# Fused vision-text encoder block: second half's turning product ahead of a block of values, moments ahead of residual rows, bias products ahead of the gather

## The reference, cut to what matters

```python
h = concatenate([h, txt], axis=1)                  # (8, 96, 192)
x = layernorm(h)
q, k, v = split(x @ Wqkv_w + Wqkv_b)               # 12 heads of 16
attn = softmax(q @ (k / 4).T + causal_mask)
attn_output = (attn @ v) @ out_w + out_b
selection = softmax((x @ sel_w + sel_b) / temperature)[..., 1:]
idx = top_k(selection, 10)                         # ten tokens of each image
y = x; y[idx] += (attn_output * selection)[idx]
h = h + y
h = h + mixture_of_experts(layernorm(h))           # 16 routed experts and a shared one
```

## Time and profile before

| | |
|---|---|
| median of 3 runs | 221.13 us (220.51 to 221.18) |
| the profiled execution, its own time | 220.96 us |
| its span, first to last instruction | 219.1 us |
| TensorE busy | 209.3 us (95%), 1433 products |
| VectorE busy | 148.6 us (68%) |
| ScalarE busy | 117.1 us (53%) |
| GpSimd busy | 36.6 us (17%) |
| chain that ended last, by engine | PE 81%, DVE 9%, ACT 3%, DMA 2%, issue 2% |

### The profile page before, as it was taken

The page is one execution under the profiler, slowest core; times in us unless marked ns, Lnnn a source line. Parts: engine busy times, 40 slices in busy tenths (PEclk is TensorE's granted clock), DMA queues, the critical chain, the costliest instruction groups (busy, mean ns, idle before and its releaser), DMA issues.

```text
span 219.1 us, 4307 instructions
## 1 busy us (share of the span) xinstructions
PE 209.3 (95%) x1433; PEld 190.2 (87%) x1433; DVE 148.6 (68%) x413; ACT 117.1 (53%) x246; POOL 36.6 (17%) x63
## 2 busy tenths in 40 slices
PE   7999999999999997999999999999999999999993
PEld 3888999888899985686877997999999999999992
DVE  0188967873566463664477699878878787878773
ACT  2157944668643746525334667266555555555552
POOL 8011006543851044040031000000000000000000
PEclk9999999999999999999999999999999999999999
DMA  6998000000000000030000001546554544444203
GB/s 222 406 405 234 0 1 4 0 3 0 3 0 0 0 3 1 1 93 6 0 3 0 0 18 27 153 149 177 146 176 138 135 153 139 138 138 138 93 0 108
DMA packets 10081, 18.69 MB, mean 85 GB/s; under 512 B 1425, under 2 KB 4641, under 8 KB 10066
## 3 DMA queue, kind: packets, MB, share of 16 engines
q1 hardware_dynamic: 9344, 16.76, 24.3%
q10 hardware_dynamic: 722, 1.74, 2.1%
HBM read 17.85 MB, written 0.64 MB: 84 GB/s over the span
## 4 chain that ended last, share of the span: by engine, by line
PE 81%; DVE 9%; ACT 3%; DMA 2%; issue 2%; POOL 1%; ACTq 1%; DVEq 0%
PE bank L544 7%; PE bank L545 6%; PE bank L547 6%; PE bank L548 6%; PE bank L546 6%; PE bank L712 4%; PE bank L581 3%; PE bank L1043 3%; PE bank L1053 3%; PE bank L1049 3%; PE bank L1044 3%; PE bank L1045 3%; DMA rows<-in_rows 2%; PE bank L691 2%; PE bank L662 2%
## 5 line engine op out<-in xcount | busy, mean ns | idle before, releaser
L1408 ACT ACTIVATE hid_s<-hid 128x384 fp32r<-128x384 f32 x34 | 17.9, 525 | 25.6 <-DVE hid L1879 25.2
L1398 ACT ACTIVATE silu<-bank,expert_raw 128x384 f32<-128x384 f32 x34 | 19.7, 579 | 10.2 <-PE bank L548 10.1
L1861 DVE SCALAR_TENSOR_TENSOR gated<-bank,expert_raw,silu 128x384 f32<-128x384 f32 x32 | 19.5, 613 | 7.3 <-PE bank L548 7.0
L1885 DVE TENSOR_TENSOR hid_s<-hid,hid_s 128x384 fp32r<-128x384 f32 x34 | 18.6, 552 | 7.8 <-ACT hid_s L1408 7.7
L544 PE MATMUL bank<-tA,ug_w 128*128 128x384 f32 x68 | 23.1, 340 | 0.1
L545 PE MATMUL bank<-tA,ug_w 128*128 128x384 f32 x68 | 22.9, 337 | 0.0
L547 PE MATMUL bank<-tB,ug_w 128*128 128x384 f32 x68 | 22.9, 337 | 0.0
L546 PE MATMUL bank<-tA,ug_w 128*128 128x384 f32 x68 | 22.9, 337 | 0.0
L548 PE MATMUL bank<-tB,ug_w 128*128 128x384 f32 x68 | 22.9, 336 | 0.0
L1879 DVE TENSOR_TENSOR hid<-w_all,gated 128x384 f32<-128x384 f32 x28 | 15.4, 552 | 0.1
L1174 ACT ACTIVATE act<-bank,cols 128x256 f32<-128x256 f32 x24 | 11.1, 472 | 7.9 <-PE bank L566 4.4
(11 more groups left out here) (356 smaller groups left out, 547.8 us busy)
## 6 DMA issues: line engine op xcount, KB each, us to landing
w_all<-routing_weights SPq DMA_DIRECT2D x14, 384.0 KB, 3.7
expert_raw<-in_experts SPq DMA_DIRECT2D x17, 256.0 KB, 3.5
expert_raw<-in_experts SPq DMA_DIRECT2D x17, 97.0 KB, 1.9
patches<-in_patches SPq DMA_DIRECT2D x3, 384.0 KB, 7.6
ff_raw<-in_ff ACTq DMA_DIRECT2D x1, 768.0 KB, 7.5
kv_raw<-in_kv SPq DMA_DIRECT2D x1, 578.0 KB, 11.8
patch_w<-in_patch_w ACTq DMA_DIRECT2D x2, 288.0 KB, 4.1
ff_raw<-in_ff SPq DMA_DIRECT2D x1, 576.0 KB, 8.6
```

The source lines that it names most:

```text
L1398: a(silu[hf][:, :], bank[3 + 2 * hf][:, 0:H2N], ACT.Silu, bias=expert_raw[:, p, BU:BU + 1]).then_inc(s[f"silu{hf}"], 1)
L1408: a(hid_s[p][:, 0, H2N * hf:H2N * hf + H2N], hid[hf][:, :], ACT.Copy)\
L1861: v.scalar_tensor_tensor((hid if first else gated)[hf][:, :], bank[4 + 2 * hf][:, 0:H2N], expert_raw[:, p, BG:BG + 1], silu[hf][:, :], ALU ...
L1885: v.tensor_tensor(hid_s[p][:, 1, tok], hid[hf][:, :], f(hid_s[p][:, 0, tok]), ALU.subtract)\
```

## The change

- TensorE: the turn of the second half goes ahead of `token_rows(3)`; the two products of `avb_all` with `out_w` go from behind the mask products to ahead of the bias row of the gather; the two fillers named `hot` there are dropped.
- ScalarE: the two row copies of the second half are put between the read-outs of images 0, 1 and 2; the rounding of the second half goes ahead of the read-outs of image 3 and of the keys.
- GpSimd: both reciprocal square roots go ahead of both sums `hx`, and both sums now come after both halves' `xn`.
- VectorE: `down_lo(0, 0)` goes from ahead of `aq_blk` to behind `hotpT`.

```diff
-    "turn_h1": 1, "vk1": 0, "psel": 0, "pickT": 1, "pick": 1, "hot": 2, "xs": 2, "aq": 0, "as0": 0,
+    "turn_h1": 1, "vk1": 0, "psel": 0, "pickT": 1, "pick": 1, "hot": 0, "xs": 2, "aq": 0, "as0": 0,
@@ GpSimd
             for hf in range(2):
                 gp.wait_ge(s["mv2_done"], hf + 1)
                 rsqrt(ve2t, mv2t, rs2t, 2 * hf, 2 * hf + 2, 128, "rs_done")
-                gp.wait_ge(s["xn_done"], hf + 1)
+            gp.wait_ge(s["xn_done"], 2)
+            for hf in range(2):
                 gp.wait_ge(s["h_rows"], 2 * hf + 2)
                 b = slice(4 * hf, 4 * hf + 4)
                 g.tensor_tensor(hx[:, b, :], h[:, b, :], xn[:, b, :], ALU.add).then_inc(s["hx_done"], 1)
@@ TensorE
             turn_logits(0)
-            token_rows(3)
             pe.wait_ge(s["xn_done"], 2)
             turn_h(xn, 1, bank[4], bank[5], "hT_ps")
+            token_rows(3)
             keys(0)
@@ TensorE
             keep_busy("hot", bank[5])
             pe.wait_ge(s["av_done"], 8)
+            pe.wait_ge(d_aq, 16)
+            pe.wait_ge(s["avb_done"], 2)
+            for ch in range(2):
+                mm(bank[7][0:SLOTS, 0:DIM], avb_all[:, ch, :], out_w[:, ch, :], start=(ch == 0), stop=False,
+                   skip_group_check=True)
...
-            pe.wait_ge(d_aq, 16)
-            pe.wait_ge(s["avb_done"], 2)
-            for ch in range(2):
-                mm(bank[7][0:SLOTS, 0:DIM], avb_all[:, ch, :], out_w[:, ch, :], start=(ch == 0), stop=False,
-                   skip_group_check=True)
@@ ScalarE
             hi_of_turned(bank[0][:, 0:H2N], bank[1][0:FB, 0:H2N], H2N, slice(0, H2N), "hT_ps", 1)
-            image_rows(0)
+            image_rows(0, 0)
+            image_rows(0, 1)
             logits_out(0)
-            for b in range(HALF_IMG):
-                values_out(b)
+            values_out(0)
+            image_rows(1, 0)
+            values_out(1)
+            image_rows(1, 1)
+            values_out(2)
+            hi_of_turned(bank[4][:, 0:H2N], bank[5][0:FB, 0:H2N], H2N, slice(H2N, T2), "hT_ps", 2)
+            values_out(3)
             keys_chunk0(0)
-            hi_of_turned(bank[4][:, 0:H2N], bank[5][0:FB, 0:H2N], H2N, slice(H2N, T2), "hT_ps", 2)
-            image_rows(1)
             logits_out(1)
@@ VectorE
             keys_chunk1(1)
-            down_lo(0, 0)
...
+            down_lo(0, 0)
```

More of the change, by code:

```diff
@@ L1306, in values_out, with image_rows @@
                     .then_inc(s["av_done"], 1)
-            def image_rows(hf):
+            def image_rows(hf, i):
                 act.wait_ge(s["mv2_done"], hf + 1)
[L1311 to L1314, removed]
+                first = HALF_IMG * hf + i
+                a(h[0:IMG_TOK, first:first + 3:2, :], x1b[64 * i:64 * i + 64, 2 * hf:2 * hf + 2, :], ACT.Copy)\
+                    .then_inc(s["h_rows"], 1)
             hi_of_turned(bank[0][:, 0:H2N], bank[1][0:FB, 0:H2N], H2N, slice(0, H2N), "hT_ps", 1)
-            image_rows(0)
+            image_rows(0, 0)
+            image_rows(0, 1)
             logits_out(0)
-            for b in range(HALF_IMG):
-                values_out(b)
+            values_out(0)
[5 more added lines that the diff above has]
+            values_out(3)
             keys_chunk0(0)
-            hi_of_turned(bank[4][:, 0:H2N], bank[5][0:FB, 0:H2N], H2N, slice(H2N, T2), "hT_ps", 2)
-            image_rows(1)
             logits_out(1)
```

## The result

The changed kernel takes 218.93 us (median of six executions) where the kernel before takes 221.16: a ratio of 0.9898, with a 95% interval of 0.9881 to 0.9915.

What follows compares the result with a forecast made beforehand. TensorE was taken to bound the kernel, busy 95% of the span and 81% of the chain. Gains of 1.28 + 0.45 = 1.73 us gave 219.4 us median; own range 219.1 to 219.7, 8 in 10 from 218.8 to 220.3.

Steps and rivals of the forecast that it cites:

- The turn, 1.28 us: TensorE, second half: turning ahead of token_rows(3) removes waits, so token_rows(4) starts at 84.24 instead of 85.52, 1.28 us gained.
- The root: GpSimd: the second half's reciprocal root, no longer behind hx, starts at 78.04 instead of 78.36, 0.32 us earlier.
- The slack of the low part: VectorE's low part of the turn: ready at 83.26, needed by logits_keys(1)'s fourth product at 83.86, 0.6 us of slack.
- ScalarE's list, costing nothing: ScalarE: row copies before image 2's read-out and the rounding moved forward cost nothing, with 0.6 us of slack.
- The bias products and the fillers, 0.45 us: TensorE, marked tokens to scores: 0.68 us of products move ahead of the gather, fillers go; scores gain 0.45 us.
- down_lo, nothing: VectorE: down_lo(0, 0) behind hotpT takes 0.5 us, done at 99.0 before the maxima at 99.7, costing nothing.
- The lock on the port pair: VectorE and GpSimd: exclusive only for VectorE operations with two SBUF inputs; down_lo then costs its bare 0.5 us.
- GpSimd's sums hold VectorE: Rival, chance 0.05: hx and avb_all shut VectorE out of the turn's low parts; fourth product 1.53 us late, 222.2 us.
- One of the moved pieces takes part back: Rival, chance 0.12: down_lo's long form costs 0.6 us, or the root brings nothing, 0.32 us; 219.7 to 220.0 us.
- Only half takes: Rival, chance 0.08: psel, after the second logits, waits on something unmoved; only the fillers' 0.45 us remain, 220.7 us.
- More than the sum: Rival, chance 0.10: selection's short steps catch up and blocks lose joints of 0.04 us; 0.3 to 0.5 more, 219.0 us.
- The clock falls, 0.03: Rival, chance 0.03: fewer fillers and a new 0.64 us gap bring TensorE 1.2 GHz; loss from 1.7 us of products.

Runs made afterwards that it cites:

- e2: Changed kernel with the two hot fillers and the bias products put back, keeping the turn's, ScalarE's and GpSimd's new order: 219.59 us, ratio 0.994 to the kernel before.
- e6: Changed kernel with GpSimd's order as before, the second half's reciprocal root behind the first hx: 219.49 us, against 220.91 for the kernel before.
- e7: Changed kernel with ScalarE's list as before, rounding behind the keys' read-out and row copies behind the rounding: 221.06 us, ratio 1.0006 to the kernel before.
- e3: Kernel before with only the bias products moved ahead of the gather and the two hot fillers dropped: 220.40 us, ratio 0.9983.
- e5: Kernel before with only the two hot fillers dropped, bias products in their old place: median 227.58 us, against 220.91 for the kernel before.
- e4: Changed kernel with down_lo(0, 0) back ahead of aq_blk: 219.14 us, against 219.27 for the changed kernel.
- the first comparison: Changed kernel as it is, first measured against the kernel before: 218.93 us against 221.16, ratio 0.9898.
- e9: Changed kernel with the two hot fillers back, ahead of the moved bias products: 219.39 us, against 220.79 for the kernel before.
- e1: Changed kernel measured again without an edit: 219.27 us against 220.86 for the kernel before, ratio 0.9925.
- e8: Changed kernel with the first three of token_rows(3)'s five products ahead of the turn, the other two behind it: 218.85 us, ratio 0.9905 to the kernel before.
- e10: Changed kernel without the eight fillers inside the gather: median 227.03 us, against 220.79 for the kernel before.
- e11: Kernel before with one hot filler instead of two, bias products in their old place: 220.69 us, against 220.79 for the kernel before.

## Why the prediction was right, point by point

- **The turn, 1.28 us.** Right in mechanism, too small in size: 1.46 us (e2). The root came 0.33 us earlier where 0.32 was said (its loss in e6: 0.35), the gap ahead of the turn measured 0.53 us as idle time, and the waits vanished. What was mis-sized are the blocks: I took 0.96, 0.92 and 0.96 us from blocks that stood behind a wait or a joint; three blocks in a row take 0.94, 0.87 and 0.86 us (81.18, 82.12, 82.99, 83.85 above). That is 0.17 us of the 0.19 us by which `token_rows(4)` came earlier than predicted; the rest is the turn, which started 0.04 us earlier after the residual sum than said and took 0.02 us longer. The slack of the low part was 0.4 us (done at 83.10, needed at 83.50), not 0.6.
- **ScalarE's list, costing nothing.** Right, but the sentence hid what it is worth: without it the turn's gain is gone and more (e7). The prediction had the reason, the rounding queued behind the keys' read-out, and priced it only together with the turn. The row copies between the read-outs cost nothing visible: image 2's read-out starts at 79.87 and the rounding waits 1.10 us behind it.
- **The bias products and the fillers, 0.45 us.** 0.41 us (e3). Up to the gather the gain is the fillers' alone (e5); the moved products take 0.71 us where 0.68 us was read, which is the difference. The second `aq_blk` was in time by 0.25 us, where 0.3 was said.
- **down_lo, nothing.** Right (e4: 0.01 us). The parts took 0.28 and 0.22 us.
- **The lock on the port pair.** The two differences of `down_lo`, with two inputs in SBUF, took 1.72 us beside GpSimd's `ug_w` (e4) and 0.41 us together without it (0.28 and 0.22 with an overlap). The turn's low parts, with one input in SBUF, took 0.56 and 0.55 us inside `hx`, as they had with GpSimd idle. This agrees with the Trainium skill ("SBUF — State Buffer", SBUF: two separate sides), whose exclusive lock concerns VectorE operations with two SBUF inputs while GpSimd reads SBUF.
- **GpSimd's sums hold VectorE.** Fell: those same low parts. One bound of it was wrong: by its own terms the fourth product starts 1.25 us after the low parts do (85.4 to 86.65), so holding VectorE begins to cost at 83.86 - 1.25 = 82.6, not at 83.2.
- **The other rivals.** *One of the moved pieces takes part back* fell with e4 and with the root's 0.33 us. *Only half takes* fell with the 1.88 us at the scores. *More than the sum* came true in a small part: blocks in a row ran shorter, as it said, and the trace has 1.87 us where the sum had 1.73; its 0.3 to 0.5 us more are only in the median of the first comparison.
- **The clock falls, 0.03.** This was the weak step. I argued from the gap of 1.14 us at 82.8, which had left the clock at full. The gap does not decide it: e5 does not have the new one and the clock fell in 5 of 6, e2 and e9 have it and the clock fell in none of 11. What TensorE does around the gather does. With the fillers dropped and nothing put there it fell in 5 of 6 executions (e5), with the bias products there in 2 of 50 (one each in the changed kernel's first six and in e3's twelve, none in e1, e4, e6, e7, e8), and with one or two fillers, wherever the bias products stood, in none of 73. The cost is about 7 us (7.0 by distance in the changed kernel's profile, 50.70 against 43.69), and about 12 us in two of e5's executions. The price in the prediction, one microsecond for each at that level, holds only for products counted at full clock: 17 us of time at 1.2 GHz cost 7.0, 0.41 for each, so 1.7 us would be lost after about 4 us of such time (an estimate from these two numbers). Whether 2 of 50 and 0 of 73 differ for a reason stays open; these numbers alone don't settle it.

## What to carry to other kernels

An earlier product is worth something only if each engine behind it takes its part out of its own queue: here the turn moved on TensorE, with the root moved on GpSimd, loses 0.56 us, and with ScalarE's list changed as well it gains 1.46 us. Real work moved into a filler's place carried the clock in 48 of 50 executions, where an empty place carried it in 1 of 6, so count a filler's removal as two prices, its own time and the clock, and measure many executions, since the second price is paid only in some. To size a chain, take block durations from blocks that stand in a row, and compare traces from a common event, not from the start of the span.

## What the runs showed of the hardware

- TensorE was granted 1.2 GHz, half of its clock, in the midst of a stretch in which the trace has it busy almost without a gap: in e5 at about 93.9, after 1.46 us of busy time in the 1.5 us from 92.0. It came back after 17 us (92.9 to 110 in the changed kernel's profile, 93.9 to 110.9 in e5), and in e10 after 10 us (95.2 to 105.4), though TensorE was busy for nearly all of that time. What stood ahead of the fall is the gather: products of ten columns each, with fillers of 512 columns between them in two of these traces and without any in e10. Why the clock falls there in one execution and not in another stays open.
- With no filler ahead of the gather 5 of 6 executions of the kernel before fell to half clock (e5), with one of 512 columns (0.23 us) none of 6 (e11).
- The busy share did not tell which execution would fall: of the 4 us from 88.0 the changed kernel's trace has TensorE busy for 3.68 us both in the execution that fell and in the one that didn't. The 0.32 us that are missing there, and 0.32 us ahead of 90.8 in e5, are no idle time of the kernel. `FILL` has a filler at that place (`pickT`), and the traces have its weight load but lack the record of its product (0.39 us at 90.44 where the kernel before has it), as here in e5's timeline of weight loads:

```profile
90.31 0.10 PEld L581 LDWEIGHTS bank<-filler 128*128 128x128 bf16 x1 [0.19 <-issue]
```
